# Moving one batch's output projection, residual and norm into the rounds of another: an attention and sparse feed-forward kernel on one core

## The reference

```python
q, k, v = x @ wq, x @ wk, x @ wv
scores = einsum('bqgrd,bkgd->bgrqk', q, k) / sqrt(16)
x = layernorm(x + einsum('bgrqk,bkgd->bqgrd', softmax(scores), v) @ wo)
inter = x @ c1.T @ c2.T                              # 512 -> 16 -> 1792
idx = argmax of each block of 32 of inter            # one of 32, 56 blocks
h = relu(w1[idx] . x);  out = h @ w2t[idx]
x = layernorm(x + out)
```

## Time and profile before

| | |
|---|---|
| three runs | 849.96, 852.8, 853.15 us; median 852.8 |
| the profiled execution | 850.92 us, of which the span of instructions is 848.9 |
| PE busy | 816.0 us, 96% |
| DVE busy | 622.4 us, 73% |
| ACT busy | 388.4 us, 46% |
| POOL busy | 292.1 us, 34% |
| PE's granted clock, mean | 0.989 |

### The profile page before, as it was taken

The page is one execution under the profiler, slowest core; times in us unless marked ns, Lnnn a source line. Parts: engine busy times, 40 slices in busy tenths (PEclk is TensorE's granted clock), DMA queues, the critical chain, the costliest instruction groups (busy, mean ns, idle before and its releaser), DMA issues. The chain is left out here.

```text
span 848.9 us, 11510 instructions
## 1 busy us (share of the span) xinstructions
PE 816.0 (96%) x4084; PEld 503.6 (59%) x4112; DVE 622.4 (73%) x804; ACT 388.4 (46%) x721; POOL 292.1 (34%) x388
## 2 busy tenths in 40 slices
PE   6999999999999999999989879999999999999995
PEld 5867433333333333333447657777777787777773
DVE  5588899999999999996036887558855795578554
ACT  4321788888888888887731022222112111122220
POOL 2212344654675465225303343342211222112221
PEclk9999999999999999999989989999999999999998
DMA  7783252344544453333225532210400040002001
GB/s 222 252 279 123 78 155 84 106 122 123 156 142 109 124 148 117 88 101 102 76 81 188 196 101 84 77 49 4 147 1 1 0 125 1 1 0 100 1 1 49
DMA packets 48224, 83.05 MB, mean 98 GB/s; under 512 B 9544, under 2 KB 13640, under 8 KB 48040
## 3 DMA queue, kind: packets, MB, share of 16 engines
q1 hardware_dynamic: 40448, 64.45, 24.5%
q0 software_dynamic: 7440, 16.76, 6.7%
q10 hardware_dynamic: 280, 1.11, 0.5%
HBM read 54.18 MB, written 28.05 MB: 97 GB/s over the span
## 5 line engine op out<-in xcount | busy, mean ns | idle before, releaser
L543 DVE TENSOR_REDUCE neg_max<-ps_pair 128x2 f32<-128x1024 f32 x256 | 301.4, 1219 | 30.6 <-PE ps_pair L641 30.6
L509 ACT ACTIVATE probs<-ps_st 128x512 f32<-128x512 f32 x512 | 265.8, 603 | 59.3 <-PE ps_st L654 58.3
L654 PE MATMUL ps_st<-q,k 50*128 50x512 f32 x512 | 185.0, 448 | 2.5 <-ACT probs L509 0.4
L654 PEld LDWEIGHTS ps_st<-q,k 50*128 50x128 f32 x512 | 83.4, 185 | 164.9 <-ACT probs L509 158.9
L892 POOL TENSOR_TENSOR g_l<-picked,g_h 128x512 fp32r<-128x512 f32 x56 | 73.0, 1303 | 250.5 <-ACT g_h L942 250.5
L641 PE MATMUL ps_pair<-k,q 48*128 48x512 f32 x512 | 149.1, 440 | 1.9 <-DVE neg_max L543 1.9
L668 PE MATMUL ps_pv<-probs,v 128*32 128x512 f32 x1024 | 136.4, 605 | 0.0
L935 ACT ACTIVATE picked<-ps_h 128x512 f32<-128x512 f32 x56 | 33.5, 598 | 182.4 <-PE ps_h L1156 182.4
L999 DVE STREAM_TRANSPOSE turned<-ps_prep 128x512 f32<-128x512 f32 x56 | 40.0, 715 | 93.3 <-PE ps_prep L1131 93.3
L1156 PE MATMUL ps_h<-xt_h,w_h 128*128 128x512 f32 x224 | 87.9, 392 | 0.5 <-ACT picked L935 0.5
L1156 PE MATMUL ps_h<-xt_l,w_h 128*128 128x512 f32 x224 | 87.5, 391 | 0.0
(11 more groups left out here) (141 smaller groups left out, 1174.6 us busy)
## 6 DMA issues: line engine op xcount, KB each, us to landing
operands<-parts POOLq DMA_DIRECT2D x20, 512.0 KB, 3.7
q<-operands SPq DMA_DIRECT2D x64, 128.0 KB, 2.5
sums<-stage SPq DMA_DIRECT2D x32, 256.0 KB, 3.1
x_raw<-xT SPq DMA_DIRECT2D x16, 256.0 KB, 5.0
k<-operands SPq DMA_DIRECT2D x64, 64.0 KB, 2.3
q<-operands SPq DMA_DIRECT2D x64, 64.0 KB, 2.6
att<-sums SPq DMA_DIRECT2D x16, 256.0 KB
yf<-x SPq DMA_DIRECT2D x4, 1024.0 KB, 5.4
```

The costliest lines, as they stand in the source:

```text
L509: nc.scalar.activation(probs[kt % 2][:, r], ps_st[i % 3][:], ACT.Exp, scale=float(HD) ** -0.5).then_inc(exp_done, 1)
L543: nc.vector.tensor_reduce(neg_max[:, at:at + 2], ps_max[pair % 2][:], AX.X, ALU.max, negate=True).then_inc(max_red, 1)
L654: nc.tensor.matmul(ps_st[i % 3][:], k_[n % QR][64 * a:64 * a + ROWS, kt * P:(kt + 1) * P], q[n % QR][64 * a:64 * a + ROWS, j, :], start=Tr ...
```

## The change

- Batch 0's `add_residual` moves into `_attend`, at the end of DVE's instructions; `project_out` there marks the end of each tile (`wo_done`). SP no longer waits in `_attend` for the last store of sums and for the load of `y0`; the first wait stands at the start of SP's next block, the second on DVE. `wo_done`, `added`, `stat_done`, `y0_in`, `stage_out` and the tile `stats` are shared by both blocks.
- Batch 3's `project_out(3, t)` become steps `late_rows(t)` of batch 0's slots 4 to 7, in a preparation bank, with their residual and statistics on DVE as part of the step. Its `scale` moves to POOL's slot 0, `high_att` to ACT's slot 1, `low_att` to POOL's slots 1 and 2; variance, root and norm to slots 8 and 9, the store to slot 10.
- Batch 1's transposes and U move from slots 2, 3, 4, 5, 8 of batch 0 to 8, 9, 10, 11, 12.
- Slot 0's `inner_up`, `first_marks` and `pick` move ahead of `project_out(2, 3)`; batch 2's residuals and norm, and batch 1's norm, are spread over the front and slots 1 to 3.
- A third buffer `y[2]`; `load_residual(2)` no longer waits. `load_w2(2)`, `(3)`, `(4)` are interleaved with the stores of batches 0 to 2. `x1_out` is one semaphore for each batch.

```diff
@@ _attend
-            for j in range(2):
-                sp.wait_ge(stage_out[j], NU // 2 * DMA)
             sp.wait_ge(rden_out, DMA * (NB - 1))
-            sp.wait_ge(y0_in, DMA)
...
+            def add_residual(t):
+                dve.wait_ge(wo_done, t + 1)
+                nc.vector.tensor_tensor(y0[:, t], ps_max[t // 2][:, t % 2], y0[:, t], ALU.add).then_inc(added, 1)
+                dve.wait_ge(added, t + 1)
+                nc.vector.bn_stats(stats[:, t], y0[:, t]).then_inc(stat_done, 1)
...
+            dve.wait_ge(y0_in, DMA)
+            for t in range(TT):
+                add_residual(t)
...
+                if third == 2:
+                    last.then_inc(wo_done, 1)
@@ _feed_forward
+    late_rows = lambda t: TT + 1 + MT + t
...
-        y = [y0, sb("yf1", [P, TT, D])]
+        y = [y0, sb("yf1", [P, TT, D]), sb("yf2", [P, TT, D])]
...
-            ahead = {2: 0, 3: 1, 4: 2, 5: 3, 8: U}
+            ahead = {2: 0, 3: 1, 4: 2, 5: 3, 8: U} if b else {8: 0, 9: 1, 10: 2, 11: 3, 12: U}
...
+            if b == 0 and 4 <= m < 4 + TT:
+                out.append((b, late_rows(m - 4)))
...
+            for j in range(2):
+                sp.wait_ge(stage_out[j], NU // 2 * DMA)
             sp.dma_start(den[:], ...)
             load_residual(1)
-            sp.wait_ge(rden_out, DMA)
-            load_att()
-            store(0, flat(x1, 0), y[0], x1_out)
             load_residual(2)
             load_w2(0)
             load_w2(1)
-            store(1, flat(x1, 1), y[1], x1_out)
+            sp.wait_ge(rden_out, DMA)
+            load_att()
+            store(0, flat(x1, 0), y[0], x1_out[0])
             load_residual(3)
-            store(2, flat(x1, 2), y[0], x1_out)
+            load_w2(2)
+            store(1, flat(x1, 1), y[1], x1_out[1])
+            load_w2(3)
+            load_w2(4)
+            store(2, flat(x1, 2), y[2], x1_out[2])
             for b in range(NB):
                 for m in range(MT):
-                    if b == 0 and m + 2 < MT:
+                    if b == 0 and 2 < m < MT - 2:
                         load_w2(m + 2)
...
@@ gpsimd
-            scale()
-            for r in range(REP):
-                low_att(r)
-            root(2)
             low_w2(0)
-            root(3)
             for b in range(NB):
                 for m in range(MT):
                     low_g(b, m)
                     if b == 0 and m + 1 < MT:
                         low_w2(m + 1)
+                    if (b, m) == (0, 0):
+                        scale()
+                    if b == 0 and m in (1, 2):
+                        low_att(2 * m - 2)
+                        low_att(2 * m - 1)
+                    if b == 0 and m in (2, 8):
+                        root(2 if m == 2 else 3)
@@ vector
+                elif s > marks(MT - 1):
+                    t = s - late_rows(0)
+                    dve.wait_ge(y_in[0], DMA)
+                    nc.vector.tensor_tensor(y[0][:, t], bank[:], y[0][:, t], ALU.add).then_inc(prep_done, 1)
+                    dve.wait_ge(prep_done, n + 1)
+                    nc.vector.bn_stats(stats[:, t], y[0][:, t]).then_inc(stat_done, 1)
...
+            variance(0)
+            norm(0)
             dve.wait_ge(den_in, DMA)
             nc.vector.reciprocal(inv_den[:], den[:]).then_inc(inverted, 1)
             for t in range(TT):
                 add_residual(1, t)
             for t in range(TT):
                 front(t)
             variance(1)
+            add_residual(2, 0)
+            add_residual(2, 1)
             front(U)
             front(marks(0))
+            pick(0, 0)
+            front(marks(1))
+            add_residual(2, 2)
+            add_residual(2, 3)
...
+                    if (b, m) == (0, 1):
+                        norm(1)
+                    if (b, m) == (0, 2):
+                        variance(2)
+                    if (b, m) == (0, 3):
+                        norm(2)
+                    if (b, m) == (0, 8):
+                        variance(NB - 1)
+                    if (b, m) == (0, 9):
+                        norm(NB - 1)
@@ tensor
             front(marks(0))
+            inner_up(0, 0, (0, 1, 2, 3))
+            first_marks(0, 0)
+            front(marks(1))
             project_out(2, 3)
-            for t in range(TT):
-                project_out(3, t)
-            inner_up(0, 0, (0, 1, 2, 3))
```

More of the change, by code:

```diff
@@ L70, in _overlays, with _attend @@
         return w_raw, w_h, w_l, x_raw, x1, v_rows, parts
-def _attend(nc, x, xT, w_qkv, wo, c1, c2, w1, dram, overlays, keep, late):
+def _attend(nc, x, xT, w_qkv, wo, c1, c2, w1, dram, overlays, keep, late, passed):
     sums, operands, maxima, rden = dram
@@ L78, in _attend @@
     att_parts2, y0, ps_max = late
+    stats, wo_done, added, stat_done, y0_in, stage_out = passed
     att_h, att_l = zip((xt_h[1], xt_l[1]), (xt_h[0], xt_l[0]), att_parts2)
@@ L711, in _, with _feed_forward @@
             weigh(NU - 1, TT - 1)
-def _feed_forward(nc, x, x1, out, w2, w2_late, sums, rden, keep, late):
+def _feed_forward(nc, x, x1, out, w2, w2_late, sums, rden, keep, late, passed):
     w1_h, w1_l, c1_h, c1_l, c2_s, ident, ident16, first, xt_h, xt_l, u, wo_h, wo_l = keep
@@ L736, in _feed_forward @@
         with ExitStack() as under:
-            att, inv = [under.enter_context(nc.sbuf_tensor(name, [P, REP, D], F32)) for name in ("att3", "inv3")]
+            att = under.enter_context(nc.sbuf_tensor("att3", [P, REP, D], F32))
         w2_h = sb("w2_h", [P, W2_OWN, D], F32R)
         den, inv_den = sb("den_last", [P, P]), sb("inv_den_last", [P, P])
+        with ExitStack() as under:
+            inv = under.enter_context(nc.sbuf_tensor("inv3", [P, REP, D], F32))
         x_sb = [sb(f"xf_sb{j}", [P, D]) for j in range(2)]
         u_next = sb("u_next", [80, S], F32R)
+        sb("at_inv", [P, S])
         turned = sb("turned", [P, S // BLK, BLK])
@@ L984, in step @@
                     elif s == 0:
-                        dve.wait_ge(wo_done, TT * (NB - 1 if b else 1))
+                        dve.wait_ge(wo_done, TT * 2)
+                        if b:
+                            dve.wait_ge(prep_mm, number(0, late_rows(TT - 1)) + 1)
                     nc.vector.tensor_copy(dst[0], src).then_inc(prep_half, 1)
@@ L1049, in norm @@
             def norm(round_):
-                buffer = y[round_ % 2 if round_ < NB else 0]
+                buffer = y[round_ % 3 if round_ < NB else 0]
                 dve.wait_ge(rstd_ready, round_ + 1)
@@ L1085, in _ @@
                     steps = slot_steps(b, m)
-                    if steps:
-                        step(*steps[0])
-                    pick(b, m)
+                    if b * MT + m:
+                        if steps:
+                            step(*steps[0])
+                        pick(b, m)
                     if len(steps) > 1:
@@ L1127, in step @@
                                                     start=(k == 0 and i == 0), stop=(k == KT - 1 and i == 2))
+                elif s > marks(MT - 1):
+                    t = s - late_rows(0)
+                    for r in range(REP):
+                        if t == 0:
+                            pe.wait_ge(att_split, r + 1)
+                        for i, (a, w) in enumerate(((att_h, wo_h), (att_h, wo_l), (att_l, wo_h))):
+                            last = nc.tensor.matmul(bank[:], a[-1][:, r, t * P:(t + 1) * P], w[:, r],
+                                                    start=(r == 0 and i == 0), stop=(r == REP - 1 and i == 2))
                 else:
@@ L1250, in build @@
         late = att_parts2, y0, [ctx.enter_context(nc.psum_tensor(f"ps_pair{j}", [P, 2, S], F32)) for j in range(2)]
-        _attend(nc, x, xT, w_qkv, wo, c1, c2, w1, (sums, operands, maxima, rden), overlays, keep, late)
-        _feed_forward(nc, x, x1, out, w2, w2_late, sums, rden, keep, late)
+        sem = lambda name: ctx.enter_context(nc.semaphore(name))
+        passed = stats, sem("wo_done"), sem("added"), sem("stat_done"), sem("y0_in"), [sem(f"stage_out{j}") for j in range(2)]
+        _attend(nc, x, xT, w_qkv, wo, c1, c2, w1, (sums, operands, maxima, rden), overlays, keep, late, passed)
+        _feed_forward(nc, x, x1, out, w2, w2_late, sums, rden, keep, late, passed)
 def kernel(L0_attn_x, L0_attn_wq, L0_attn_wk, L0_attn_wv, L0_attn_wo, L0_ffn_c1_w, L0_ffn_c2_w, L0_ffn_w1,
```

91 lines of the change are left out of this document (36 added, 55 removed).

## The result

The changed kernel takes 852.42 us (median of 20 runs), the kernel before 851.09 in the 20 runs beside it: a ratio of 1.0015, 95% interval 1.0008 to 1.0021. That is 0.15% slower, where 0.56% faster was predicted. One run of the changed kernel at 4145 us is left out of the ratio. The median before was 852.8 when the prediction was made (three runs), so its gain of 4.8 us would be 846.3 against the 851.09. The profiled execution took 852.66 us, its span 850.5.

A forecast was written before the change was run, and what follows sets the result against it. PE was taken as the bound, with only handover gaps changeable: 16.0 us before, 11.2 after, gain 4.8, so 846.1 us profiled or 848.0 against the 852.8 median (0.56% faster). Range 840 to 853 us.

The forecast's parts named there:

- marks 0: Front, before slot 0's `first_marks`: PE waits for DVE's marks step, ready at 464.5; gap 0.35 us.
- what bounds the kernel: Opening passage: PE is the bound; only the handover from attention, 16.0 us beyond PE's own work, can change.
- Part 1, the entry: Attention's end: residual moved, block no longer waits for last store; gap 1.6 us, no low clock.
- The rival of a fall there: Entry: clock already falls in the 1.6 us gap, 2.6 us more, gain 2.2, 850.6 us; chance 0.10.
- Part 2, the front: From 437.1 to slot 0's end: batch 1's residual lands at 444.1, gap 0.15; before `first_marks`, gap 0.35 us.
- Part 3: Slots 0 to 2: DVE's chain makes PE wait 0.4 us for g; the old 3.26 and 1.36 go.
- Part 4, the queue: Slot 3: w2(3) queued behind `store(1)` delays the relu; gap 5.2 us, plus 2.4 of low clock.
- a hidden wait: Slot 3: w2(3) comes before about 479.4, no gap or clock fall; gain 13.5, 839.3 us; chance 0.15.
- a held clock: Slot 3: clock holds through the queue gap; gain 7.2, 845.6 us; chance 0.06.
- a slow `store(1)`: SP queue: `store(1)` lands as slowly as `store(0)`, w2(3) 9.5 us later; gain -4.7, 857.5 us; chance 0.07.
- Part 5, slot 4: Same queue wait again, w2(5) behind `store(2)`: gap 1.1 us (0 to 2.0).
- Slots 8 to 12: Batch 1's transposes and U moved here; DVE lags 2.2 us at most, costed at nothing.

The follow-up runs named there:

- with 512 bytes: Changed kernel with 416 unused bytes behind `stats`, so `w1_h` and later tiles are shifted by 512 bytes in all: 847.04 us, ratio 0.9949.
- with 128 bytes: Changed kernel with 32 unused bytes behind `stats`, so `w1_h` and later tiles are shifted by 128 bytes in all: 849.97 us, ratio 0.9985.
- the two mended orders: Changed kernel with SP's loads of w2 blocks 3 and 5 ahead of the stores, 844.28 us; or with ACT's `high_w2` behind relu and `high_g`, 844.47 us.
- the w2 run: Kernel before with 96 unused bytes ahead of `w2_h`, moving it and the tiles after it: ratio 1.0041.
- `stats` behind w1: Changed kernel with w2 loads ahead of the stores and `stats` allocated behind `w1_l`, no pad: 843.09 us, ratio 0.9899.
- at the entry without the third buffer: Kernel before with only batch 0's residual and the last-store wait moved, `stats` padded to 512 bytes, two y buffers: 850.49 us, ratio 0.9988.
- The run with 96 bytes: Kernel before with an unused 96-byte tile ahead of `w1_h`, nothing else: 855.25 us, ratio 1.0043.
- the kernel before with 256: Kernel before with 256 unused bytes ahead of `w1_h`: ratio 0.9997.
- the kernel before with the pad ahead of `turned`: Kernel before with 96 unused bytes ahead of `turned`, moving only other engines' tiles and `mask_t`: ratio 0.9999.

## Why the prediction was wrong, step by step

The terms, in us. Slots 3 and 4 are named as in the prediction: the gaps stand in front of `inner_up` of slots 3 and 5. The low clock is the length of the 13 matmuls from the gap to `first_marks`, less the 3.1 that the same stretch takes at the full clock (504.10 to 507.21 in the run with 512 bytes).

| | predicted | changed kernel | with 512 bytes |
|---|---|---|---|
| entry | 1.6 | 1.52 | 1.52 |
| front | 0.15 | 0.67 | 0.67 |
| marks 0 | 0.35 | 0.21 | 0.27 |
| g of slot 1 | 0.4 | 0 | 0 |
| slot 3, relu | 5.2 | 5.58 | 5.61 |
| low clock behind it | 2.4 | 490.70 - 486.25 - 3.1 = 1.3 | 491.02 - 485.30 - 3.1 = 2.6 |
| slot 4, relu | 1.1 | 2.41 | 1.15 |
| low clock behind it | 0 | 509.76 - 505.07 - 3.1 = 1.6 | 0 |
| sum | 11.2 | 13.3 | 11.8 |
| longer matmuls | 0 | 4.7 | 0 |

- **The step that failed** is in the passage on what bounds the kernel: "The change adds no matmul and removes none [...], so the new time is the old one with other gaps". The number of matmuls was right and their length was taken for granted. 84 ns a slot over the 50 slots behind slot 5 is 4.2 us (from there to the last `first_marks` 323.98 us in the changed kernel, 319.80 with 512 bytes), and the six slots ahead of them, at the same 84 ns, hold 0.5. That is the whole difference: with the 512 bytes, the distance from attention to the last gap is 396.33 us, 4.0 less than before, where the terms give 16.0 - 11.8 = 4.2 and the prediction 4.8. No rival named it. The diff showed it, as one line in the allocations.
- **Part 1, the entry,** right: 1.52 against 1.6, clock held. The rival of a fall there is refuted by the 1.00 from 437.
- **Part 2, the front:** residual 1 landed at 444.5 (I had 444.1), and PE's gap is 0.67 where I had 0.15. DVE ended its four adds at 449.9, 2.3 us behind PE's 48 matmuls where I had 1.5, so the 0.17 that I kept from the kernel before did not carry over. It cost 0.5 us.
- **Part 3** right to 0.5 us in sum, with the gap before slot 1's g at nothing instead of 0.4; `norm(1)` at 475.42 for 3.87 us against 475.45 and 3.8.
- **Part 4, the queue,** right in place and cause: store at 479.32 (479.2), w2(3) seen by ACT 5.8 us behind it (5.4), PE at 486.25 (485.85). The rivals of a hidden wait, a held clock and a slow `store(1)` are all refuted. What the wait cost in whole the two mended orders show, some 8.5 us each. `store(1)` landed 5.0 us after its issue. The Trainium skill (DMA: Bandwidth & Descriptors, Queues, rings and completion order) says that on each DMA engine descriptors are consumed in ring order; the 256 KB behind the store's 1 MB, 5.3 us from their own issue where 2.8 was the median, agree.
- **Part 5, slot 4,** right in mechanism, off in size: 2.41 for 1.1, and a second low clock of 1.6 that I had at 0. The size hangs on the first low clock: T is when the relu came, and a PE that is slow for longer behind it waits less for the next. Gap and first low clock together are 1.3 + 2.41 = 3.7 us here, 1.5 + 2.18 = 3.7 with 128 bytes and 2.6 + 1.15 = 3.8 with 512; predicted were 3.5. Why the first low clock was shorter here than with 512 bytes no run shows, and so the size of the second gap was luck either way. But with 2.41 the clock fell once more, with 2.18 (128 bytes) and 1.15 it did not. So the fall cost 1.6 us in one and nothing in the others.
- **Slots 8 to 12** right: no gap there.

What stays open: why an address costs a matmul anything, and whether it is the distance of the two operands that counts. Against that being all: in the steady slots `inner_up` gets longer from 228.7 ns to 230.2 in the w2 run and to 231.4 with `stats` behind w1, where neither of its operands moved. Attention itself ended between 433.8 and 436.5 us in these kernels, over nearly unchanged code; I did not find from what, and every sum of terms above is counted from its end.

## What to carry to other kernels

A new tile ahead of TensorE's operands is a change to every matmul: allocate it behind all of them (behind w1 alone did not do), or fill it up to a multiple of 256 bytes, of which 256 and 512 were run here, and compare the slot in a stretch that has no gaps (here 5.967 against 6.051 us) before explaining anything else. Where a load is moved behind a store in one queue, follow both queues, the DMA's and that of the engine that converts the load: what stands behind the conversion in program order waits too, and either order can be mended. The gain of a wait removed is what is left when the next chain arrives (8.5 us of 11 here, 1 of 5 at the entry without the third buffer).

## What the runs showed of the hardware

- The pace of these 128x512 matmuls that overlap with no gap depends on the byte address of their operands in a partition: 228.7 ns from start to start in `inner_up` with tiles at the old addresses or 256 or 512 bytes further, 234.1 at 96. The Trainium skill (Advanced Engine Details and Errata, SBUF Cachelines) speaks of 16-byte lines and of accesses that hit the same one; 96 and 128 are multiples of 16, so if lines of 16 bytes were all that counted, neither shift would cost anything. The run with 96 bytes cost 4.2 us, and it decides.
- A shift of either operand alone costs: 5.4 ns a matmul with the held one moved (`inner_up` of the changed kernel), 1.5 with the streaming `w2_h` moved (`inner_down` of the w2 run, 232.2 against 230.7 ns). A shift of tiles that only other engines read (and of `mask_t`) costs nothing, ratio 0.9999.
- The clock fell after an idle time of 2.41 us and not after 2.18 (128 bytes), 2.10 (the kernel before with 256), 1.55 or 1.52; after one of 2.23 us in the kernel before with the pad ahead of `turned`, with a second gap close behind, it read 0.70 in the next microsecond. In the 5.58 us gap it fell while PE was idle (0.88 in the last microsecond of it), behind the 2.41 us gap only when PE had worked for a microsecond again (1.00 from 505, 0.62 from 506, 0.50 from 507).
- The low clock cost 1.3 us behind one gap of 5.58 us and 2.6 behind another of 5.61, in kernels that differ only in addresses.
